# Causal attention on one core: two sums of exponentials joined on VectorE before the row-sum products

## What is computed

```python
xn = _layernorm(x)
scores = jnp.einsum('bhqd,bhkd->bhqk', q, k) * scale
scores = jnp.where(causal, scores, jnp.finfo(scores.dtype).min)
probs = jax.nn.softmax(scores, axis=-1)
attn = jnp.einsum('bhqk,bhkd->bhqd', probs, v)
x = x + attn_projected + ffn(xn)
```

## Time and profile before

| What | us |
|---|---|
| median of 3 runs | 1812.9 |
| the profiled execution | 1812.03 |
| its span | 1810.2 |
| attention | 178 to 731 |
| a middle pair of heads | 69.34 |

### The profile page before, as it was taken

The page is one execution under the profiler, slowest core; times in us unless marked ns, Lnnn a source line. Parts: engine busy times, 40 slices in busy tenths (PEclk is TensorE's granted clock), DMA queues, the critical chain, the costliest instruction groups (busy, mean ns, idle before and its releaser), DMA issues.

```text
span 1810.2 us, 29086 instructions
## 1 busy us (share of the span) xinstructions
PE 1778.5 (98%) x10560; PEld 1355.3 (75%) x10560; DVE 1140.9 (63%) x1738; ACT 714.2 (39%) x1171; POOL 735.7 (41%) x728
## 2 busy tenths in 40 slices
PE   7999999999999999999999999999999999999998
PEld 6886666666566665788888888888888888888887
DVE  5526666666666667776676666567567567666654
ACT  3323666666665666232232223222323223322322
POOL 1432678778778776132222122222222222212221
PEclk9999999999999999999999999999999999999999
DMA  8785043143242202511100110110110110010002
GB/s 284 219 235 146 10 104 79 33 104 67 44 102 57 55 22 68 177 46 36 35 23 12 35 34 1 35 35 0 35 35 0 35 35 24 11 35 0 1 1 93
DMA packets 75617, 108.60 MB, mean 60 GB/s; under 512 B 24912, under 2 KB 44992, under 8 KB 72384
## 3 DMA queue, kind: packets, MB, share of 16 engines
q1 hardware_dynamic: 75520, 107.34, 21.6%
HBM read 74.04 MB, written 29.59 MB: 57 GB/s over the span
## 4 chain that ended last, share of the span: by engine, by line
PE 59%; DVE 0%; ACT 0%; issue 0%; ACTq 0%
PE p_up L51 6%; PE p_v L51 6%; PE p_up L50 6%; PE p_v L50 6%; PE p_up L49 6%; PE p_v L49 6%; PE p_s L51 6%; PE p_s L50 6%; PE p_s L49 6%; PE p_s L344 0%; PE p_s L338 0%; PE p_s L339 0%; PE p_v L338 0%; PE p_v L339 0%; PE p_v L344 0%; PE p_up L338 0%
## 5 line engine op out<-in xcount | busy, mean ns | idle before, releaser
L1364 POOL TENSOR_SCALAR poly<-poly 128x1024 f32<-128x1024 f32 (+1 forms) x65 | 72.0, 1108 | 801.3 <-ACT poly L1321 801.3
L891 DVE TENSOR_REDUCE max_part<-p_s 128x1 f32<-128x512 f32 x384 | 248.1, 685 | 144.6 <-PE p_s L987 144.2
L726 POOL TENSOR_TENSOR e_sum<-e_sb 128x512 f32<-128x512 f32 (+1 forms) x244 | 290.8, 1219 | 108.5 <-PE p_o L1055 91.2
L808 ACT ACTIVATE e_sb<-p_v 128x512 f32<-128x512 f32 (+3 forms) x427 | 216.4, 552 | 128.3 <-PE p_v L1015 68.9
L1427 DVE SCALAR_TENSOR_TENSOR inter<-inter,gate 128x1024 f32<-128x1024 f32 (+1 forms) x65 | 78.6, 1209 | 241.1 <-ACT inter L1327 240.2
L49 PE MATMUL p_v<-xn_hi,w_hi 128*128 128x512 f32 x512 | 199.2, 389 | 0.0
L50 PE MATMUL p_v<-xn_lo,w_hi 128*128 128x512 f32 x512 | 199.2, 389 | 0.0
L51 PE MATMUL p_v<-xn_hi,w_lo 128*128 128x512 f32 x512 | 199.2, 389 | 0.0
L49 PE MATMUL p_up<-xn_hi,w_hi 128*128 128x512 f32 x512 | 199.2, 389 | 0.0
L50 PE MATMUL p_up<-xn_lo,w_hi 128*128 128x512 f32 x512 | 199.2, 389 | 0.0
L51 PE MATMUL p_up<-xn_hi,w_lo 128*128 128x512 f32 x512 | 199.2, 389 | 0.0
(11 more groups left out here) (189 smaller groups left out, 3404.4 us busy)
## 6 DMA issues: line engine op xcount, KB each, us to landing
k_stack<-qk_scratch SPq DMA_DIRECT2D x42, 256.0 KB, 7.2
qk_scratch<-out_hi SPq DMA_DIRECT2D x32, 256.0 KB, 2.7
qk_scratch<-out_lo SPq DMA_DIRECT2D x32, 256.0 KB, 3.3
q_stack<-qk_scratch SPq DMA_DIRECT2D x24, 256.0 KB, 6.4
xn_lo_scratch<-xn_lo SPq DMA_DIRECT2D x4, 1024.0 KB, 5.2
v_stack<-in_gate_up_s SPq DMA_DIRECT2D x64, 64.0 KB, 2.3
xn_lo<-xn_lo_scratch SPq DMA_DIRECT2D x4, 1024.0 KB, 13.9
scales<-in_gate_up_s SPq DMA_DIRECT2D x64, 64.0 KB, 2.4
```

The source lines that it names most:

```text
L726: nc.gpsimd.tensor_tensor(*operands(k, i), ALU.add).then_inc(pool_summed, 1)
L808: nc.scalar.activation(e_sb[:, x % E_BUFS, 0:w], bank_st(x)[:, 0:w], ACT.Exp, scale=SCALE).then_inc(exp_done, 1)
L891: nc.vector.reduce_max(part, p_s[:, slot[n] % S_BUFS, 0:w], AX.X).then_inc(maxed, 1)
L1364: nc.gpsimd.tensor_scalar(part_of(poly, h, parts), part_of(poly, h, parts), GELU_A, 1.0, ALU.mult, ALU.add).then_inc(poly_done, 1)
```

## The change

After its units but the last of an off-diagonal group, VectorE waits until the group's additions are done and adds the first sum to the second for each head (`join_sums`, two additions of 128x512 f32). In a group without units it does so after its own additions. A new semaphore `joined` counts these. `row_sums` off the diagonal waits for `joined` and multiplies only the second sums: 4 matmuls in place of 8. `needs` lets an addition take a first sum's buffer when that sum is joined, and any other when its row sums are done, as before.

```diff
+    JOINED_TO = list(itertools.accumulate(0 if DIAG[GS * k % NS] else 2 for k in range(NG)))
...
             if x is None:
-                return 0, made[k, i - 2][1]
-            return (sum_group[n - SUM_BUFS] + 1 if n >= SUM_BUFS else 0), 0
+                return None, made[k, i - 2][1]
+            if n < SUM_BUFS:
+                return None, 0
+            group = sum_group[n - SUM_BUFS]
+            if not DIAG[GS * group % NS] and n - SUM_BUFS < first_sum[group] + 2:
+                return (joined, JOINED_TO[group]), 0
+            return (rows_done, group + 1), 0
...
                         if free:
-                            dve.wait_ge(rows_done, free)
+                            dve.wait_ge(*free)
...
+            def join_sums(k):
+                if DIAG[GS * k % NS]:
+                    return
+                dve.wait_ge(pool_summed, added_to[k][0])
+                if added_to[k][1]:
+                    dve.wait_ge(vector_summed, added_to[k][1])
+                for a in range(2):
+                    other, here = ((first_sum[k] + 2 * j + a) % SUM_BUFS for j in range(2))
+                    nc.vector.tensor_tensor(e_sum[:, here, :], e_sum[:, here, :], e_sum[:, other, :],
+                                            ALU.add).then_inc(joined, 1)
...
                 for n in units:
+                    if n == units[-1]:
+                        join_sums(k)
                     unit_max(n)
...
                 sum_steps(k)
+                if not units:
+                    join_sums(k)
...
             def row_sums(k):
                 p, s = divmod(GS * k, NS)
-                pe.wait_ge(pool_summed, added_to[k][0])
-                if added_to[k][1]:
-                    pe.wait_ge(vector_summed, added_to[k][1])
+                if not DIAG[s]:
+                    pe.wait_ge(joined, JOINED_TO[k])
+                else:
+                    pe.wait_ge(pool_summed, added_to[k][0])
+                    if added_to[k][1]:
+                        pe.wait_ge(vector_summed, added_to[k][1])
...
                 else:
-                    for j in range(2):
-                        for h in range(2):
-                            for a in range(2):
-                                last = add(a, h, 0, HALF, total(2 * j + a, h * HALF, (h + 1) * HALF), False)
+                    for h in range(2):
+                        for a in range(2):
+                            last = add(a, h, 0, HALF, total(2 + a, h * HALF, (h + 1) * HALF), False)
```

More of the change, by code:

```diff
@@ L16 @@
+import itertools
 import numpy as np
@@ L508, in attention @@
         vector_summed = sem("vector_summed")
+        joined = sem("joined")
         rows_done = sem("rows_done")
@@ L722, in sum_steps @@
                         if free:
-                            pool.wait_ge(rows_done, free)
+                            pool.wait_ge(*free)
                         if earlier:
```

## The result

The changed kernel takes 1802.4 us (median of 6 runs, 1800.5 to 1805.1) against 1812.55 for the kernel before on the same chip: a ratio of 0.9947, 95% interval 0.9936 to 0.9957, so 0.53% faster. The forecast was 1806.5. The span of the profiled execution is 1798.7 us, 11.5 shorter than the one before.

What follows compares the result with a forecast made beforehand. TensorE was taken to bound the kernel. Net of additions delaying it, six middle pairs gave -2.1 us, the first -1.0, the last -0.3 and its tail -2.5: -5.9 from 1812.0 or 1812.9, so 1806.5; range 1800 to 1811.

Steps and rivals of the forecast that it cites:

- The bound: TensorE limits attention; halving 48 off-diagonal row-sum blocks from 16 to 8 instructions removes 0.445 us each, 21.4 us.
- The release: First-sum buffers come free at the join, ending TensorE's wait at place 5: 1.18 us in each of six pairs, 7.1 us.
- The additions and their turns: VectorE's 96 additions alternate with GpSimd at SBUF: 1.3 to 3.8 us a pair of additions, mean addition above 1.1 us.
- The hold: TensorE waits for late last maxima behind the additions: 3.5 us per middle pair of heads, against 3.85 gained.
- the six places: Off-diagonal groups, numbered 1, 3, 4, 6, 7 and 8 among the ten (0 to 9) of a pair of heads.
- place 4: Off-diagonal group: GpSimd's last add ends 0.5 us into the gap, last maximum 1.3 us late, TensorE held 0.6 us.
- Place 6: Off-diagonal group with a shorter gap: last maximum 2.1 us late, TensorE held 1.35 us.
- its tail: End of the last pair, no scores left: 2.2 us from five groups plus 1.7 of stalls less 1.4, net -2.5 us.
- the stall of 1.02 us behind the copy-out: Last pair: TensorE waits behind a copy-out delayed by VectorE; expected to go, part of 1.7 us of stalls.
- the layout: One pair of heads with additions placed among GpSimd's work in turns: 2.7 us a pair of additions, near break-even.
- The light one: Rival: turns are rare, a pair of additions takes under 2 us, the whole 30.2 us comes: 1783 us; chance 0.20.
- The heavy one: Rival: additions cost the long price everywhere, 3.5 us a pair, TensorE held 6.9 us per pair: 1829 us; chance 0.25.

Runs made afterwards that it cites:

- one-operand run: Changed kernel with VectorE's two additions replaced by maxima reading one SBUF operand, first sums left out of the row sums: 1786.8 us, ratio 0.9861.

## Why the prediction was right, and where its sizes were off

**The bound.** TensorE, as said: 8 matmuls less in 48 places come out of the time at 0.44 us each in a middle pair (0.445 forecast), shown by the two one-operand runs.

**The release.** The waits of GpSimd for row sums fell from 91.2 to 16.1 us ("under 30"), and the row sums of place 5 wait for nobody. The term of the sum was mis-sized, though: I put 1.18 us a pair on that wait, and the release brought 0.6. This is the step that failed: I measured the delay between the starts of two blocks, 2.96 us at place 5 and 1.78 at place 2. But at place 2, where nobody is late, the row sums on the diagonal start before the last products and are mixed with them; at place 5 they wait, and all products are done by then. So a late start is partly made good within the block. The delay has to be taken up to the next other work, the first score behind the block. These rows of the kernel before belong to place 2 (the first three) and place 5:
```profile
538.45 0.39 PE L1041 MATMUL p_o<-e_sb,v_stack 128*32 128x256 f32 x2
538.49 0.39 PE L1055 MATMUL p_o<-e_sum,ones 128*32 128x128 f32 x4
...
539.42 0.33 PE L987 MATMUL p_s<-k_stack,stack_lo 96*128 96x128 f32 x1
...
560.50 0.50 PE L987 MATMUL p_s<-k_stack,stack_lo 96*128 96x512 f32 x1
```
From the row sums of the place before to this score it is 539.42 - 536.47 = 2.95 us at place 2 and 560.50 - 556.95 = 3.55 at place 5. The difference is 0.60 us, just what the release brought. In the run with the old block length and one operand, place 5 takes 2.95 too. No other engine has to be called in.

**The additions and their turns.** The mean is 1159 ns in the rows of attention and the median 1215, forecast "above 1.1 us"; GpSimd's full additions rose from a mean of 1287 to 1323 ns. The mechanism is shown: with one operand from SBUF the same work holds nobody. The rule weighed there, of the Trainium skill, page SBUF — State Buffer, section "SBUF: two separate sides", is borne out: 673 to 687 ns for all 96 with one SBUF operand, up to 1774 with two.

**The hold.** Forecast 0.1, 0, 0.6, 1.35, 1.0 and 0.45 us at the six places, 3.5 in all; measured against the one-operand run it is 0, 0, 0, 0.8, 1.0 and 0.2, 2.04 in all. Places 6 and 7 were the right ones. The step that failed most is place 4. I let GpSimd end the group's sums 0.5 us into the gap; they were ready, the join started with no wait at 543.43 and took 2.11 us, and the gap of 2.4 us held it. Place 6 was put too high by almost as much, 1.35 for 0.8.

**The sum.** A middle pair: 3.24 us gained (3.85 forecast) less 2.04 (3.5), so 1.2 in place of 0.35; six of them 7.1 us in place of 2.1. That is nearly the whole difference from the forecast. The first pair gained 1.8 (forecast 1.0), the last 2.1 (forecast 2.8, of them 2.5 in its tail). In the last pair the stall of 1.02 us behind the copy-out is gone as I had it, but the row sums that waited 0.66 us for VectorE's adds still wait 0.62, and the last ones 0.85 where it was 0.33. I also had no term for the granted clock: in the stretch in which it fell, from the row sums of place 3 to those of place 4, the changed kernel takes 8.48 us and the one-operand run, at full clock, 7.09. In every run with two-operand joins the mean clock of the last pair is 0.96 or 0.97, in the others 1.00; why it falls there stays open, since TensorE is busy about as little at that spot in the one-operand run (3.15 of the 4 us ahead of the row sums of place 3).

That the point came within 4.1 us is partly luck. Two errors of size, 0.6 and 1.5 us a pair, worked against each other: with the right 0.6 for the release and the hold as forecast, the sum would have been about 1810. The break-even was put at 3.0 us for a pair of additions, the layout at 2.7; the measured mean is 2 x 1.16 = 2.3.

**The rivals.** The light one, 1783, is what the kernel would have without turns: 1786.8 was measured, and most of the 3.8 us between them is the oversized release (six times 0.58). The heavy one was not seen, but the two runs that push the join out of its gap are slower than the kernel before, 1843.6 and 1895.4.

## What to carry to other kernels

Work moved from a full engine to an idle one should go into a gap where that engine waits for the full one anyway: here the same additions made the kernel 0.5% faster ahead of the last maximum and 1.8% slower behind it. Before such work is placed, ask which other engine reads SBUF at that moment, and try one wide instruction in place of two, because each may have to wait for a whole instruction of the other engine. Here that was worth 11 us with the normalisations moved, and nothing clear of noise without. And look at what delays the data that the gap needs: here two normalisations a pair that could as well run elsewhere were worth 10 us, but only once the additions were one instruction, and nothing at all before the change. And when a wait is priced from a trace, measure up to the next work of another kind, not from start to start of the block that waited: here the second gave 1.18 us and the first 0.60, and 0.6 was what it brought.

## What the runs showed of the hardware

A VectorE maximum over 128x512 f32 from SBUF is not disturbed by GpSimd's additions (673 to 687 ns, 96 of them), nor is a subtraction with one operand in PSUM that writes to SBUF (680 to 693 ns, 12 of the 32 wholly beside a GpSimd instruction); an addition with both operands in SBUF is (678 to 1774 ns), and the waiting stands in the profile as the instruction's own length, not as idle time. Two of VectorE's back to back let one of GpSimd's in between (3.39 us for 1.3 us of work), one of twice the width lets none in (2.22 for 1.2).

When maxima held TensorE to 3.77 busy us out of 6, its granted clock went to 0.50 for the 6 us that followed, though it was busy in all of them, and then came back. The run with the old release lost 83 us where 28 to 43 were expected of the waits; by the estimate above, 0.08 of 620 us, the clock could be nearly all of the difference, but it was not separated from holds that were longer than expected. In the changed kernel the clock fell once, to 0.56 and 0.59 over 4 us, behind 4 us in which TensorE was busy 3.16.
